# State space stage: places of the output products and of GpSimd's products by C, and the front's loads by score tile

## The reference, cut to what matters

```python
x = x + xattn(layernorm(x), ctx)        # 16 batches, 128 tokens, width 512; context of 2048 keys; 16 heads
x = x + mamba_block(layernorm(x))       # the stage that the change touches, then an MLP
x = x + moe(layernorm(x))               # shared expert plus a weighted expert

# inside the mamba block, for each channel d (1024) and state n (16), over t (128 tokens):
xz = Z @ in_proj_w.T;  u, z = split(xz);  u = silu(causal_conv4(u))
dt, B, C = split(u @ x_proj_w.T);  dt = softplus(dt @ dt_proj_w.T + b)
h[t] = exp(dt[t] * A[d, n]) * h[t-1] + dt[t] * B[t, n] * u[t]
y[t] = sum_n h[t] * C[t, n] + D * u[t]
out  = (y * silu(z)) @ out_proj_w.T
```

## Time and profile before

| | us |
|---|---|
| median of 3 runs | 4062.3 (4059.43 to 4064.45) |
| the profiled execution | 4066.44 |
| its span, first to last instruction | 4064.6 |
| PE busy | 3858.2 (95%) |
| DVE busy | 2817.6 (69%) |
| ACT busy | 1739.4 (43%) |
| GpSimd busy | 1246.6 (31%) |
| state space steps 0 to 7, first scan to last gate | 2479.3 to 3508.1 |

### The profile page before, as it was taken

The page is one execution under the profiler, slowest core; times in us unless marked ns, Lnnn a source line. Parts: engine busy times, 40 slices in busy tenths (PEclk is TensorE's granted clock), DMA queues, the critical chain, the costliest instruction groups (busy, mean ns, idle before and its releaser), DMA issues. The chain is left out here.

```text
span 4064.6 us, 83414 instructions
## 1 busy us (share of the span) xinstructions
PE 3858.2 (95%) x34816; PEld 2799.1 (69%) x34816; DVE 2817.6 (69%) x2977; ACT 1739.4 (43%) x3466; POOL 1246.6 (31%) x587
## 2 busy tenths in 40 slices
PE   8999999999999999999999998999999997699998
PEld 6777877777777777787777775455545553387876
DVE  5667666667766766765766766999999998754433
ACT  2324424423433432442442346777777776322221
POOL 1111111011111111101101105888888888410000
PEclk9999999999999999999999998999999999899999
DMA  4110111010011011011001022210121101220000
GB/s 153 38 42 28 38 45 39 28 50 31 28 50 43 28 38 43 28 38 53 31 28 50 30 73 84 58 58 16 58 58 58 55 19 47 80 73 22 32 22 16
DMA packets 96789, 183.73 MB, mean 45 GB/s; under 512 B 8337, under 2 KB 12817, under 8 KB 96434
## 3 DMA queue, kind: packets, MB, share of 16 engines
q1 hardware_dynamic: 96434, 178.27, 13.4%
HBM read 152.82 MB, written 25.43 MB: 44 GB/s over the span
## 5 line engine op out<-in xcount | busy, mean ns | idle before, releaser
L241 POOL TENSOR_TENSOR c_lo<-c_raw,c_hi 128x2048 fp32r<-128x2048 f32 x64 | 294.7, 4605 | 1973.4 <-DVE c_hi L343 1973.4
L431 DVE TENSOR_TENSOR prob_sums<-prob_sums,probs 128x1024 f32<-128x1024 f32 x480 | 566.6, 1222 | 122.1 <-ACT probs L316 122.1
L983 POOL TENSOR_TENSOR b_drive<-b_dt_u,b_bc 128x1024 f32<-128x1024 f32 x256 | 600.7, 2357 | 137.8 <-PE b_y L1420 103.9
L404 DVE TENSOR_REDUCE max_parts<-scores 128x2 f32<-128x1024 f32 x512 | 601.8, 1218 | 40.4 <-PE scores L568 40.4
L316 ACT ACTIVATE probs<-scores 128x512 f32<-128x512 f32 x1024 | 529.0, 603 | 221.9 <-PE scores L599 221.9
L396 DVE SCALAR_TENSOR_TENSOR k_lo<-scores,bk_sb,k_hi 128x512 fp32r<-128x512 f32 x256 | 192.3, 751 | 564.7 <-ACT k_hi L301 564.7
L1420 PE MATMUL b_y<-b_drive,b_ident 128*128 128x512 f32 x1024 | 500.9, 618 | 86.3 <-DVE b_drive L1283 64.7
L1272 DVE TENSOR_TENSOR_SCAN b_decay<-b_decay,b_drive 128x1024 f32<-128x1024 f32 x216 | 494.2, 2288 | 26.1 <-ACT b_decay L1138 21.0
L301 ACT ACTIVATE k_hi<-scores,bk_sb 128x512 fp32r<-128x512 f32 x256 | 176.4, 689 | 603.6 <-PE scores L520 603.6
L309 ACT COPY v_sb<-scores 128x512 f32<-128x512 f32 x240 | 141.1, 588 | 668.5 <-PE scores L520 668.5
L1138 ACT ACTIVATE b_decay<-b_dt,b_a 128x254 f32<-128x254 f32 x1024 | 425.2, 461 | 0.4
(11 more groups left out here) (222 smaller groups left out, 6462.0 us busy)
## 6 DMA issues: line engine op xcount, KB each, us to landing
c_raw<-in_ctx SPq DMA_DIRECT2D x64, 1024.0 KB, 5.2
b_bc<-bc_scratch SPq DMA_DIRECT2D x128, 256.0 KB, 4.3
q_scratch<-v_sb SPq DMA_DIRECT2D x4, 1024.0 KB, 4.3
q_raw<-q_scratch SPq DMA_DIRECT2D x16, 256.0 KB, 5.1
q_raw<-in_x SPq DMA_DIRECT2D x16, 256.0 KB, 2.9
x_scratch<-q_raw SPq DMA_DIRECT2D x16, 256.0 KB, 5.8
attn_scratch<-attn_out_sb SPq DMA_DIRECT2D x16, 256.0 KB, 2.0
b_attn<-attn_scratch SPq DMA_DIRECT2D x8, 512.0 KB, 5.4
```

The lines of the kernel that those rows point to most:

```text
L241: pool.tensor_tensor(c_lo[:, slot], c_raw[:], c_hi[:, slot].bitcast(F32), ALU.subtract).then_inc(c_lo_ready, 1)
L404: dve.tensor_reduce(max_parts[:, g, 2 * pair:2 * pair + 2, s], max_banks[:, 2 * pair:2 * pair + 2, :], AX.X, ALU.max).then_inc(max_taken, 1)
L431: dve.tensor_tensor(part, part, probs[:, u % 4], ALU.add).then_inc(summed, 1)
L983: pool.tensor_tensor(drive[:, m % 4], dt_u[:, 2 * p:2 * p + 2, :].unsqueeze(1).to_broadcast([P, SG, 2, T]), bc[:, g, 0].unsqueeze(2).to_br ...
```

## The change

Four edits in `mamba`, and one in the attention's SP program that the first needs:

- SP's loads of the front are cut (`wo` in halves, `w_in` in four chunks for each half), and each waits for `scores_ready` of one more score tile of the last attention batch: `wo` for tiles 0 and 1, `x1` and the convolution's weights for 2, the x half of `w_in` for 3 to 6, the small weights for 7, the z half for 8 to 11.
- PE's output products stand after units 27, 29, 31 instead of 27, 28, 30.
- ACT's first rounding stands after unit 23 instead of 22.
- GpSimd's products by C are those of units 10, 11, 12, 16, 19 instead of 10, 11, 12, 13, 19, and in the last step those of 10, 13, 16, 19, 22, 25, 28. The count that others wait for (`wait_for_c_product`) is adapted.

```diff
--- before.py
+++ after.py
@@ -223,7 +223,10 @@
                 sp.dma_start(attn_dram[batches - 1], out_sb[:]).then_inc(attn_stored, 16)
                 sp.wait_ge(attn_stored, 16 * (batches + 1))
 
-            return store_last
+            def wait_for_scores(t):
+                sp.wait_ge(scores_ready, (batches - 1) * tiles + t + 1)
+
+            return store_last, wait_for_scores
 
         def run_gpsimd(pool):
             pool.memset(ident[:], 0.0).then_inc(ident_ready, 1)
@@ -700,17 +703,17 @@
     assert steps % 2 == 0 and rank % 32 == 0
 
     PE_HEADS, PE_OUT_LAST, PE_TURN, PE_IN_X, PE_X, PE_DT = (0, 2), 3, 6, (8, 9, 10, 12), 16, (18, 20)
-    PE_IN_Z, PE_OUT = (13, 14, 15, 17, 22, 23, 25, 26), (27, 28, 30)
+    PE_IN_Z, PE_OUT = (13, 14, 15, 17, 22, 23, 25, 26), (27, 29, 31)
     POOL_DT_U1, POOL_DT_H1, POOL_DT_U2, POOL_DT_U3, POOL_RSTD, POOL_OUT = 0, 3, 6, 8, 5, 11
     POOL_LOW = (25, 31)
     POOL_DT_H0 = 30
     ACT_LOG1, ACT_SQUARES, ACT_XN, ACT_XN_T, ACT_SCALE, ACT_TAP, ACT_U = 1, 8, 7, 9, 13, (11, 12, 14, 16), 17
     ACT_Z, ACT_DBC, ACT_ABS, ACT_EXP = (18, 20, 26, 29), 19, (21, 24), (22, 25)
-    ACT_ROUND, ACT_LOG0, ACT_GATE = (22, 29), 27, 4
+    ACT_ROUND, ACT_LOG0, ACT_GATE = (23, 29), 27, 4
     ACT_FIRST_Z = (0, 1, 2)
     DVE_SUM, DVE_X1, DVE_CONV = 5, (2, 4), (11, 12, 13, 15)
     LATE_GROUPS = 3
-    POOL_C = (10, 11, 12, 13, 19)
+    POOL_C, POOL_C_LAST = (10, 11, 12, 16, 19), (10, 13, 16, 19, 22, 25, 28)
     C_BEHIND = 2
 
     bc_dram = nc.dram_tensor("bc_scratch", (steps, 2 * states, T), F32).ap()
@@ -812,13 +815,15 @@
         def z_bank(n):
             return 1 if n == 0 else 2
 
-        on_vector = [m for m in range(units) if m not in POOL_C]
+        def on_pool(i):
+            return POOL_C_LAST if i == steps - 1 else POOL_C
 
         def wait_for_c_product(eng, i, m):
-            if m in POOL_C:
-                eng.wait_ge(y_part_pool, i * len(POOL_C) + POOL_C.index(m) + 1)
+            if m in on_pool(i):
+                eng.wait_ge(y_part_pool, i * len(POOL_C) + on_pool(i).index(m) + 1)
             else:
-                eng.wait_ge(y_part, i * len(on_vector) + on_vector.index(m) + 1)
+                made = [n for n in range(m + 1) if n not in on_pool(i)]
+                eng.wait_ge(y_part, i * (units - len(POOL_C)) + len(made))
 
         def run_steps(eng, front, body, finish):
 
@@ -830,22 +835,30 @@
             body(steps - 1, 1, False, True)
             finish()
 
-        def run_sync(sp, store_last):
+        def run_sync(sp, store_last, wait_for_scores):
             sp.sem_inc(zm_stored, 32)
             sp.dma_start(attn[:], attn_v[0]).then_inc(attn_loaded, 16)
-            sp.dma_start(wo[:], wo_t.rearrange("(k p) o -> p k o", p=P)).then_inc(wo_loaded, 16)
+            wo_v = wo_t.rearrange("(k p) o -> p k o", p=P)
+            w_in_v = w_in_t.rearrange("(k p) o -> p k o", p=P)
+            for half_k in range(2):
+                wait_for_scores(half_k)
+                ks = slice(half_k * chunks // 2, (half_k + 1) * chunks // 2)
+                sp.dma_start(wo[:, ks], wo_v[:, ks]).then_inc(wo_loaded, 16)
+            wait_for_scores(2)
             sp.dma_start(x1[:], x_v[0]).then_inc(x_loaded, 16)
-            w_in_v = w_in_t.rearrange("(k p) o -> p k o", p=P)
-            for part in range(2):
-                cols = slice(part * inner, (part + 1) * inner)
-                sp.dma_start(w_in[:, :, cols], w_in_v[:, :, cols]).then_inc((x_half_loaded, z_half_loaded)[part], 16)
-                if part == 0:
-                    sp.dma_start(conv_w_sb[:], conv_w).then_inc(x_half_loaded, 16)
-                    sp.dma_start(conv_b_sb[:], conv_b).then_inc(x_half_loaded, 16)
+            sp.dma_start(conv_w_sb[:], conv_w).then_inc(x_half_loaded, 16)
+            sp.dma_start(conv_b_sb[:], conv_b).then_inc(x_half_loaded, 16)
+            for k in range(chunks):
+                wait_for_scores(3 + k)
+                sp.dma_start(w_in[:, k, 0:inner], w_in_v[:, k, 0:inner]).then_inc(x_half_loaded, 16)
+            wait_for_scores(3 + chunks)
             for dst, src in ((w_x[:], w_x_t.rearrange("(k p) o -> p k o", p=P)),
                              (w_dt[0:rank, :], w_dt_t), (w_dt[rank:rank + 1, :], dt_b),
                              (a_neg[:], a_log), (d_sb[:], d_skip)):
                 sp.dma_start(dst, src).then_inc(loaded, 16)
+            for k in range(chunks):
+                wait_for_scores(4 + chunks + k)
+                sp.dma_start(w_in[:, k, inner:], w_in_v[:, k, inner:]).then_inc(z_half_loaded, 16)
             store_last()
             sp.dma_start(norm_sb[:], norm_w.partition_broadcast(P)).then_inc(out_loaded, 16)
             sp.dma_start(w_out[:], w_out_t.rearrange("(k p) o -> p k o", p=P)).then_inc(out_loaded, 16)
@@ -902,7 +915,7 @@
 
             run_steps(sp, front, body, finish)
 
-        X_HALF_LOADED, Z_HALF_LOADED, LOADED, OUT_LOADED = 3 * 16, 16, 5 * 16, 2 * 16
+        WO_LOADED, X_HALF_LOADED, Z_HALF_LOADED, LOADED, OUT_LOADED = (16 * n for n in (2, 2 + chunks, chunks, 5, 2))
 
         def run_gpsimd(pool):
             pool.memset(ident[:], 0.0).then_inc(ready, 1)
@@ -984,7 +997,7 @@
                         drive[:, m % 4], dt_u[:, 2 * p:2 * p + 2, :].unsqueeze(1).to_broadcast([P, SG, 2, T]),
                         bc[:, g, 0].unsqueeze(2).to_broadcast([P, SG, 2, T]), ALU.mult
                     ).then_inc(drive_ready, 1)
-                    if m - C_BEHIND in POOL_C:
+                    if m - C_BEHIND in on_pool(i):
                         c_product(i, m - C_BEHIND)
                     if m == POOL_DT_U1:
                         make_dt_u(i, par, 1)
@@ -1124,7 +1137,7 @@
                     p, g = m // groups, m % groups
                     if not first or m >= 2:
                         k, n = (i, m - 2) if m >= 2 else (i - 1, units + m - 2)
-                        if n in POOL_C:
+                        if n in on_pool(k):
                             act.wait_ge(scanned, k * units + n + 1)
                         else:
                             wait_for_c_product(act, k, n)
@@ -1268,7 +1281,7 @@
                     dve.wait_ge(decay_ready, i * units + m + 1)
                     dve.wait_ge(drive_ready, i * units + m + 1)
                     increments = drive[:, m % 4].rearrange("p n c t -> p (n c t)")
-                    state = increments if m in POOL_C else decay[:, m % 2]
+                    state = increments if m in on_pool(i) else decay[:, m % 2]
                     dve.tensor_tensor_scan(state, decay[:, m % 2], increments,
                                            0.0, ALU.mult, ALU.add).then_inc(scanned, 1)
                     if g == 0:
@@ -1276,7 +1289,7 @@
                             end_pair(i, par, p - 1)
                         elif not first:
                             end_pair(i - 1, 1 - par, pairs - 1)
-                    if m not in POOL_C:
+                    if m not in on_pool(i):
                         dve.wait_ge(scanned, i * units + m + 1)
                         if p == 0:
                             dve.wait_ge(bc_loaded[g], i * 32 + 32)
@@ -1304,7 +1317,7 @@
         def run_tensor(pe, values_last, attention_done):
             pe.sem_inc(summed, 4)
             pe.wait_ge(ready, 7)
-            pe.wait_ge(wo_loaded, 16)
+            pe.wait_ge(wo_loaded, WO_LOADED)
 
             def project_heads(j, b, first):
                 if b == 0:
@@ -1949,8 +1962,8 @@
 
         @block.sync
         def _(sp):
-            store_last = attention[0](sp)
-            state_space[0](sp, store_last)
+            store_last, wait_for_scores = attention[0](sp)
+            state_space[0](sp, store_last, wait_for_scores)
 
         @block.gpsimd
         def _(pool):
```

## The result

The changed kernel takes 4031.95 us (median of 4 runs, 4028.01 to 4033.0), the kernel before 4062.61 beside it (4059.43 to 4064.45); the ratio is 0.9924, with a 95% interval of 0.9906 to 0.9941. The forecast was 4022, 4006 to 4042. The profiled execution took 4028.01 (span 4026.2) against 4066.44 (4064.6) before.

What follows compares the result with a forecast made beforehand. PE and DVE were taken to share the bound of a middle state space step, each idle about 9 us waiting for the other. Terms 8.2 + 15.4 + 8.8 - 1.2 + 9.5 = 40.7 us off 4062.3 gave 4022, range 4006 to 4042.

Steps and rivals of the forecast that it cites:

- Step 1: Last attention batch: loads released by score tile stop PE's instruction loads queueing behind the weights; 8.2 us saved.
- Step 2: State space step boundaries: output products at 27, 29, 31 remove DVE's 2.75 us gate wait; 15.4 us saved.
- PE alone decides the boundary: Rival at the step boundaries: output products gain only 2.75 us, rounding's gain holds; 4035 us, chance 0.17.
- Step 3: Unit 23 of seven state space steps: later ACT rounding removes DVE's 1.25 us wait for decay 23; 8.8 us saved.
- Step 4: GpSimd's product 16 for 13: net 0 in a middle step, 1.2 us lost in step 0 at sum 16.
- slower rival: Unit 16 in seven steps: GpSimd's product two operations (4.7 us) late, costing 33 us; 4095 us, chance 0.04.
- four signs of being wrong: PE waiting for GpSimd at sum 16, steps over 127 us, last-step GpSimd waits of DVE, issue stops at 180 GB/s.
- Step 5: Last step: seven spaced GpSimd products remove 7.9 us of waits and 2.4 of DVE's products; 9.5 us saved at PE's end.

Runs made afterwards that it cites:

- E1: Kernel before with only the front's loads cut and released by score tile: 4057.35 us, ratio 0.9984 to the kernel before.
- E12: Changed kernel with the later loads again in one burst as before, all else as changed: 4043.61 us, ratio 0.9946 to the kernel before.
- E10: Kernel before with its one burst of loads held back until score tile 6 is ready: 4061.1 us, ratio 1.0.
- E2: Kernel before with only the output products moved, to after units 27, 29, 31: 4047.76 us, ratio 0.9957.
- E3: Kernel before with only ACT's first rounding moved, to after unit 23: 4052.34 us, ratio 0.9971.
- E4: Kernel before with only GpSimd's product by C at 16 instead of 13, in all eight steps: 4059.08 us, ratio 0.9997.
- E5: The changed kernel run again without any edit: 4032.85 us, ratio 0.9931 to the kernel before.
- E9: Changed kernel with the last step's products by C at 10, 11, 12, 16, 19 and output products after 17, 19, 24: 4027.89 us, ratio 0.9915.
- E6: Changed kernel with the last step's products by C at 10, 11, 12, 16, 19 as in the other steps: 4027.97 us, ratio 0.9919.
- E7: Changed kernel with the last step's output products after 27, 28, 30 as before: 4033.45 us, ratio 0.9933.
- E8: Changed kernel with the last step's output products after 17, 19, 24: 4028.7 us, ratio 0.9919.
- E11: Changed kernel with a spare, unread PE product after each of sums 4 to 26 of the last step: 4028.04 us, ratio 0.9916.

## Why the prediction was right, and where it was off

**Step 1, loads: right in kind, 6.5 of 8.2 us.** E1 gives 7.1 alone, E12 takes 6.9 back, E10 moves the stops with the burst, and in it the instruction packets start up to 7.1 us apart instead of 4.0, each stop ending 1.3 to 1.4 us after one of them landed. So it is shown that these stops come with the burst and end behind such packets. That PE lacks its instructions in them was my reading in the prediction and is not shown: no trace names the engine that a packet of q8 is for. Why such a packet starts late, no run shows either. What was over-sized is the assumption that 180 GB/s, against the 404 of the earlier trace rows, costs nothing: 1.0 us of "issue" in the two score products and 0.3 in the value products is left, and the tiles span 44.9, not 42.7. A second effect I had only as a row: a granted clock of 0.50 just behind the stops. Executions differ in it: in E2 it stood at 0.50 from 2390 to 2412 and the front took 123.0, in E10 it stood at 1.00 from 2385.99 to 2420 and the front took 110.3. The six profiles with the burst have fronts of 109.3 (E3), 110.3, 110.7 (E4), 113.8 (before), 114.1 (E12) and 123.0; the eight with spread loads have 106.2 to 108.2. So what the loads are worth in one execution lies between 1 and 17 us, and the 6.5 of the table is one draw. The runs of the kernels with the burst mostly scatter more (E12 by 15 us, E1 by 4.4).

**Step 2, output products: right.** Forecast 15.4, E2 15.4 over the seven boundaries; wait of the head sum forecast 0.6, measured 0.73 to 0.75. The rival "PE alone decides the boundary" (4035) fell: its steps would have stayed near 128.7, or at 127.9 with the 0.78 that E2's expectation gives it.

**Step 3, rounding: right, slightly small.** 8.8 forecast, 10.2 in E3 (1.4 per step where the wait was 1.25; where the rest comes from is open).

**Step 4, product 16: right.** 0 per middle step (measured +0.05), +1.2 in step 0 (measured +1.1, with a wait of 0.72 for GpSimd at sum 16). The slower rival (GpSimd late for unit 16 in every step) fell: in the changed kernel's middle steps PE waits for it at sum 16 in one alone, 0.72 us in the odd step below. That was one of the prediction's four signs of being wrong, as were "issue" stops at 180 GB/s and waits of DVE for GpSimd in the last step (0.8 left, once); these three came, in small size.

**Steps 2 to 4 together** lose a little: alone they sum to 15.4 + 10.2 - 1.5 = 24.1 over steps 0 to 6, together 21.7 came. One part was forecast without a price: scan 22 waits 1.41, and scan 20 another 0.5 to 0.8, for decays that stand behind PE's solid chain. The other is one odd step (step 3), 126.85 us in the changed kernel, E5 and E9, while its neighbours and E6, E7, E8, E11, E12 have 125.2 to 125.5:

```profile
2881.22 3.78 PE L1433 MATMUL b_y<-b_drive,b_ident 128*128 128x512 f32 x4 [2.67 <-DVE b_drive L1296]
...
2888.88 0.69 DVE L1247 TENSOR_TENSOR b_gate<-b_y,b_gate 128x512 f32<-128x512 f32 x1 [2.05 <-PE b_y L1433]
```

That sum comes after the same 2.67 us of idle time in each of steps 1 to 6, and takes 2.87, 1.98, 3.78, 1.98, 3.60 and 3.05 us there. In E6's same step it takes 3.41, with the turn and the next sum behind it at full speed (1.04 and 1.88); in the odd step they are slow as well (1.92 and 2.34). So gate 8 waits 2.05 instead of 0.43, and with DVE that late PE's sum 16 waits for GpSimd:

```profile
2926.11 1.98 PE L1433 MATMUL b_y<-b_drive,b_ident 128*128 128x512 f32 x4 [0.72 <-POOL b_drive L968]
```

Without the odd step the shortfall is 1.0 to 1.5 (E6, E7, E8, E12), with it 2.4.

**Step 5, the last step: the step that failed.** The prediction read the 7.9 us of DVE's waits for GpSimd and at gate 16 as queue order and called them gone by spacing. DVE's waits for GpSimd did go (1.4 left over the whole stage), but gates 16 and 24 wait 2.36 and 2.37:

```profile
3406.94 8.45 PE L1433 MATMUL b_y<-b_drive,b_ident 128*128 128x512 f32 x12 [3.14 <-POOL b_drive L968]
...
3415.43 0.69 DVE L1247 TENSOR_TENSOR b_gate<-b_y,b_gate 128x512 f32<-128x512 f32 x1 [2.36 <-PE b_y L1433]
...
3436.96 5.38 PE L1433 MATMUL b_y<-b_drive,b_ident 128*128 128x512 f32 x8 [2.76 <-POOL b_drive L968]
...
3442.38 0.69 DVE L1247 TENSOR_TENSOR b_gate<-b_y,b_gate 128x512 f32<-128x512 f32 x1 [2.37 <-PE b_y L1433]
3469.12 0.69 DVE L1247 TENSOR_TENSOR b_gate<-b_y,b_gate 128x512 f32<-128x512 f32 x1 [3.24 <-PE b_y L1433]
```

I priced a sum at 1.8 us everywhere. Three sums took 8.45 here and two 5.38 (granted clock 0.64 and 0.68), where eight products take 3.70 at clock 1.00 and so twelve, as an estimate, 5.5: 2.9 and 1.7 us too long, ahead of exactly the two gates. In each case PE had just waited 3.14 and 2.76 us for one of GpSimd's products. The kernel before was no different (7.21 us at clock 0.75), so its wait of 2.60 at gate 16 was partly slow PE as well, 1.7 us of it by the same estimate, which spacing did not remove:

```profile
3442.57 7.21 PE L1420 MATMUL b_y<-b_drive,b_ident 128*128 128x512 f32 x12 [2.21 <-POOL b_drive L955]
```

The 7.1 us that the last step and tail did give are not the spacing's: E6 has 6.9 without it, and product 16 alone gave 5.9. So the term came near its number in part by luck: the seven spaced products that it is built on gave nothing. How far the clock falls changes from one execution to the next: between gates 16 and 24 it is 26.95, 31.04 or 31.41 us with the same program (changed kernel, E7, E12), at granted clocks of 0.94, 0.78 and 0.78. There the length follows the clock. It does not do so everywhere: between gates 8 and 16 of the last step, with GpSimd's products by C bunched, the clock was 0.77 in E1 and E10, 0.83 in the kernel before and 0.89 in E2 and E3, and the stretch took 31.3, 31.3, 31.4, 31.5 and 31.6 us. There GpSimd is busy for 30.1 of 31.3 us (E1), and PE's clock does not set the length. That GpSimd's spaced products call the clock down is argued from the rows, since E11, meant to show it, did not isolate it.

A further 2.4 us was foreseen and remains: the output product of unit 31 stands ahead of the last one. E8 and E9, with the products at 17, 19, 24, where PE is idle, have a tail of 4.48; in the medians E9 gains nothing over E6 by it.

**The median.** The forecast was 4021.6 from the traces' sum. Of the 10 us between that and 4032, 5.4 are the terms above (1.7, 1.3, 2.4). The rest is the step from a trace to a median: the changed kernel's profiled execution is its fastest run, 3.9 us under its median, and the kernel before's lay 4.1 over its own, which the forecast carried over. That is 8.0, less the 3.1 of "all else". The changed kernel's last step at the 0.78 of E7 and E12 would cost 4 to 5 us by their lengths, which is also how far the median lies above those of E6, E8, E9 and E11 (4027.9 to 4028.7); that this is the cause stays open, as no unprofiled run shows its clock by stretch.

## What to carry to other kernels

Here the waits at a boundary where two engines meet could be priced to a tenth or two of a microsecond from the order of time, as long as one also asks what the freed engine meets next. A load whose data are wanted later should go out in pieces, tied to the progress of the work that it runs beside: here, during a burst of 6.78 MB at 382 to 404 GB/s, an engine that does not touch the data yet stood at "issue" for 1.0 to 1.9 us at a time, and with the same loads in pieces for 0.2 to 0.9. Where TensorE waits again and again between a few products, price the next ones at both granted clocks that the traces show (four products took 1.98 us at 1.00 and 3.78 at 0.50), and ask whether TensorE ends last there. Compare two versions only after the same stretch has been looked at in more than one execution.

## What the runs showed of the hardware

- TensorE stopped at "issue" for 0.9 to 1.1 and 1.6 to 2.0 us, 9 to 10 and 15 to 17 us after 6.78 MB of loads in one burst began (404 GB/s in the kernel before, 382 in E10), and in the kernel before and E12 for 1.6 and 1.9 once more. Spread out (235 GB/s between 2370 and 2388 in the changed kernel, where the kernel before has 353) the stops were 0.2 to 0.9 us, and in E1 there was one, of 0.58.
- The stops ended 1.2 to 1.6 us after a 16 KB packet of the instruction queue landed (28 stops, 14 traces). In E10's burst these packets started 7.1 and 6.4 us apart, ahead of it 4.0; the two late ones took 0.96 and 1.01 us, three ahead of the burst 0.93 to 1.41.
- The granted clock in one stretch of identical work (36 products, PE idle for 9 to 10 us of it) was 0.94 in one execution and 0.78 in two others, for 27.0 and 31.0 to 31.4 us.
- The four products of one sum, each time after the same wait of 2.67 us, took from 1.98 to 3.78 us in six steps of one execution (the changed kernel), the 1.98 at a granted clock of 1.00 and the 3.78 at 0.50.
- A spare product after each sum raised the last step's clock from 0.94 to 0.98 and left its length at 112.8 us.
